# A four-layer gated transformer on one core: half of the expert gates spread by DMA instead of by TensorE

## What is computed

```python
x = x + tanh(g_xattn[L]) * attention_L(layernorm(x), ctx)
x = x + tanh(g_ffn[L])   * experts_L(layernorm(x))

# layer 0: 32 experts of width 64 (and 8 that do nothing), 6 of 40 per token
y = silu(x @ Wg.T) * (x @ Wu.T) @ Wd.T;        out += gate[e][:, None] * y
# layer 1: 16 experts of width 64, 2 per token, and a shared one of width 352
# layer 2: 31 experts of width 128, 3 per token, and a shared one of width 128
h = gelu(x @ W1 + B1);                         out += gate[e][:, None] * (h @ W2 + B2)
# layer 3: 8 experts of width 256 with relu, 2 per token
# layer 3's attention alone takes an integer mask over (query, key)
```

## Time and profile before

| | |
|---|---|
| runs shown, median (range) | 738.41 us (736.62 to 739.43) |
| the profiled execution: its own time | 738.34 us |
| its span | 736.5 us |
| PE busy | 652.4 us, 89% of the span |
| DVE busy | 531.7 us, 72% |
| ACT busy | 378.5 us, 51% |
| POOL busy | 270.8 us, 37% |
| DMA | 28.50 MB, mean 39 GB/s |
| spread matmuls, L675 | 150, first and last in the expert stages of layers 0 and 3 |

### The profile page before, as it was taken

The page is one execution under the profiler, slowest core; times in us unless marked ns, Lnnn a source line. Parts: engine busy times, 40 slices in busy tenths (PEclk is TensorE's granted clock), DMA queues, the critical chain, the costliest instruction groups (busy, mean ns, idle before and its releaser), DMA issues.

```text
span 736.5 us, 11957 instructions
## 1 busy us (share of the span) xinstructions
PE 652.4 (89%) x3653; PEld 457.8 (62%) x3653; DVE 531.7 (72%) x1298; ACT 378.5 (51%) x652; POOL 270.8 (37%) x463
## 2 busy tenths in 40 slices
PE   2787679998899988998999899999988899979997
PEld 2575547775676655675566546777766676645764
DVE  5482788887877537987864569888877988544886
ACT  1544254543467632553466337777744565622774
POOL 7723356663210003363111216666742000020673
PEclk9997689999999998999999999999999999998999
DMA  8211042110000010010000301111100010100111
GB/s 284 92 73 72 0 157 73 43 44 0 2 4 31 18 59 0 23 44 11 1 4 21 99 0 38 36 43 43 37 7 1 4 32 3 32 0 1 37 43 36
DMA packets 24087, 28.50 MB, mean 39 GB/s; under 512 B 4002, under 2 KB 19938, under 8 KB 24036
## 3 DMA queue, kind: packets, MB, share of 16 engines
q1 hardware_dynamic: 24036, 27.87, 12.2%
HBM read 22.22 MB, written 5.24 MB: 37 GB/s over the span
## 4 chain that ended last, share of the span: by engine, by line
PE 68%; DVE 20%; ACT 4%; issue 4%; POOL 2%; DMA 1%; DVEq 0%; SPq 0%; ACTq 0%; POOLq 0%
PE PS L653 10%; PE PS L654 10%; PE PS L655 10%; PE PS L675 4%; PE PS L879 4%; PE PS L516 4%; PE PS L788 3%; PE PS L862 3%; DVE consts L1503 2%; DVE negmax L1497 2%; DVE qst L1457 1%; PE PS L894 1%; DVE hid_lo L1412 1%; PE PS L859 1%; DVE xn L1224 1%
## 5 line engine op out<-in xcount | busy, mean ns | idle before, releaser
L414 POOL TENSOR_TENSOR wpair<-ring,ones_col 128x128 fp32r<-128x128 f32 (+1 forms) x150 | 78.7, 525 | 139.2 <-PE PS L655 98.7
L1406 DVE TENSOR_TENSOR pT<-pT,PS 128x512 f32<-128x512 f32 x150 | 102.5, 684 | 28.7 <-ACT pT L1050 22.8
L1149 ACT ACTIVATE pT<-PS 128x512 f32<-128x512 f32 x160 | 92.1, 592 | 49.2 <-PE PS L862 39.7
L1412 DVE TENSOR_TENSOR hid_lo<-pT,hid_hi 128x512 fp32r<-128x512 f32 x150 | 112.0, 746 | 2.3 <-ACT hid_hi L1057 1.4
L416 POOL TENSOR_TENSOR wpair<-ring,wpair 128x128 fp32r<-128x128 f32 (+1 forms) x150 | 103.5, 690 | 11.7
L1057 ACT ACTIVATE hid_hi<-pT 128x512 fp32r<-128x512 f32 x150 | 93.8, 625 | 12.4 <-DVE pT L1406 12.1
L653 PE MATMUL PS<-hid_hi,wpair 128*128 128x512 f32 x150 | 86.6, 577 | 5.8 <-DVE hid_lo L1412 5.8
L653 PE MATMUL PS<-xhi,wpair 128*128 128x512 f32 x204 | 85.3, 418 | 2.5 <-DVE pT L1406 1.9
L1050 ACT ACTIVATE pT<-PS,ring 128x512 f32<-128x512 f32 x96 | 65.9, 689 | 36.6 <-PE PS L655 36.6
L654 PE MATMUL PS<-xlo,wpair 128*128 128x512 f32 x204 | 82.5, 404 | 0.0
L655 PE MATMUL PS<-xhi,wpair 128*128 128x512 f32 x204 | 82.4, 404 | 0.0
(11 more groups left out here) (239 smaller groups left out, 1289.6 us busy)
## 6 DMA issues: line engine op xcount, KB each, us to landing
ring<-in_mlp SPq DMA_DIRECT2D x48, 128.5 KB, 2.1
ring<-in_glu SPq DMA_DIRECT2D x27, 192.0 KB, 2.4
keys<-qst SPq DMA_DIRECT2D x18, 256.0 KB, 2.0
kz<-keys SPq DMA_DIRECT2D x36, 128.0 KB, 3.1
qst<-kfull SPq DMA_DIRECT2D x96, 4.0 KB
...
```

The costliest lines, as they stand in the source:

```text
L1149: act.activation(pT[:, w % 8, :], PS[:, 2 + w % 2, :], ACT.Exp, scale=sc).then_inc(A["p"], 1)
L1406: dve.tensor_tensor(hid[:, hf, :], src[:, hf, :], PS[:, 6 + hf, :], ALU.mult).then_inc(M["hid"], 1)
L1412: dve.tensor_tensor(hid_lo[:, kept, :], hid[:, kept % 2, :], hid_hi[:, kept, :].bitcast(f32), ALU.subtract).then_inc(M["lo"], 1)
```

## The change

From entry 2 on in every layer, the gate of the second token half no longer comes through a spread matmul.

- PE transposes the second half's rows of `wtab` as f32 (4 transposes into bank 7, right after the old ones), ACT copies them out as `gate_rows` (32 rows of 512), between its copy of `wT` and its first activation.
- SP waits for `gate_rows`, writes them to DRAM, waits until that has landed, and then brings a row back onto 64 partitions with each DMA, two per entry: for entries 2 and 3 at once, and for entry e+4 right behind the ring load of that entry. These waits and DMAs stand ahead of `stack_keys` and of the mask loads on SP.
- DVE's multiplication of odd units from entry 2 on reads the gate from SBUF (`gate_slot`) and not from PSUM. Even units, and entries 0 and 1, stay as they were. That leaves out 14, 9, 30 and 14 spread matmuls in layers 0 to 3, 67 in all.
- `start_results` (the old L697 and L701) moves from ahead of the first spread to behind up(2) and spread(2). PE's second spread waits for `gate_rows`.
- The masks are prepared in six pieces, one behind each of units 24 to 29 of layer 0 (of 32), and no longer in layer 1's routing. `negk` moves into `ctx_tok`.
- The filler before `turn_weights` goes from 30 to 22 matmuls in layer 1, stays 30 in layer 2 and goes to 15 in layer 3.
- Some loads share a semaphore (`ld_gate` goes into `ld_bias`, `ld_out1` to `ld_out3` into `ld_out`, `kz_set` into `set_pool`); the loads stay as they were.

```diff
+        gate_rows = pT[0:EP, 7, :]
+        gate_own = sb("gate_own", [P, HALF])
+        gate_slot = [consts[:, C_DFT:C_DFT + HALF], consts[:, C_DFT + HALF:C_DFT + 2 * HALF], consts[:, C_BAND:C_BAND + HALF],
+                     gate_own[:, :]]
+        gd = [nc.dram_tensor(f"gates{L}", (EP, HALF), f32, kind="Internal").ap() for L in range(4)]
...
-        negk = sb("negk", [P, TB, S], bf16)
+        negk = ctx_tok[:, 6:8, :].rearrange("p a n -> p (a n)").bitcast(bf16).rearrange("p (k n) -> p k n", k=TB)
...
+        rows_out, rows_saved = sem("rows_out"), sem("rows_saved")
+        gate_in = [sem(f"gate_in{k}") for k in range(RING)]
+        by_pe = 2
+        gates_before = [[sum(len([e for e in range(by_pe, ROUTE[M]["ENT"]) if e % RING == k]) for M in range(L))
+                         for k in range(RING)] for L in range(4)]
...
+                def spread_gate(e, k):
+                    for side in range(2):
+                        row = gd[L][bass.ds(2 * e + side, 1), :] if glu else gd[L][bass.ds(e, 1), :]
+                        sp.dma_start(gate_slot[k][side * 64:side * 64 + 64, :],
+                                     row.broadcast_to([64, HALF])).then_inc(gate_in[k], 16)
+
                 if L == 0:
                     save_keys()
+                sp.wait_ge(rows_out, L + 1)
+                sp.dma_start(gd[L], gate_rows[:, :]).then_inc(rows_saved, 16)
+                sp.wait_ge(rows_saved, 16 * (L + 1))
+                for e in range(by_pe, RING):
+                    spread_gate(e, e)
...
                         sp.dma_start(ring[:, k, 0:cols], w[RING * i + RING + k, :, :]).then_inc(ring_in[k], 16)
+                        spread_gate(RING * i + RING + k, k)
                 for e in range(n - n % RING, n):
                     sp.wait_ge(M["y"], 2 * (e - RING) + 2 + UP_AHEAD)
                     sp.dma_start(ring[:, e % RING, 0:cols], w[e, :, :]).then_inc(ring_in[e % RING], 16)
+                    spread_gate(e, e % RING)
...
+                    pe.wait_ge(kv_out, len(chunks))
+                for i in range(4):
+                    mm = pe.transpose(PS[0:EP, 7, i * P:(i + 1) * P], wtab[:, 4 + i, :], ident)
+                mm.then_inc(rt["tr"], 1)
...
-                    keep_busy(7, 30)
+                    keep_busy(7, (0, 22, 30, 15)[L])
                 turn_weights(L)
-                for hf in range(NHALF):
-                    if glu:
-                        mm = pe.matmul(PS[:, hf, :], zerob[:, 0:P], zerob[:, :], start=True, stop=False,
-                                       skip_group_check=True)
-                    else:
-                        for j in range(PARTS):
-                            mm = pe.matmul(PS[:, hf, :], b2part[L][:, j, :], wT[:, hf * HALF:(hf + 1) * HALF],
-                                           start=(j == 0), stop=False, skip_group_check=True)
-                    mm.then_inc(M["y"], 1)
+                def start_results():
+                    for hf in range(NHALF):
+                        if glu:
+                            mm = pe.matmul(PS[:, hf, :], zerob[:, 0:P], zerob[:, :], start=True, stop=False,
+                                           skip_group_check=True)
+                        else:
+                            for j in range(PARTS):
+                                mm = pe.matmul(PS[:, hf, :], b2part[L][:, j, :], wT[:, hf * HALF:(hf + 1) * HALF],
+                                               start=(j == 0), stop=False, skip_group_check=True)
+                        mm.then_inc(M["y"], 1)
+
                 if glu:
                     pe.wait_ge(astep, (1, 4)[L])
                 if L == 0:
                     pe.wait_ge(kv_out, len(chunks))
-                for hf in range(NHALF):
-                    spread(hf, 0, hf)
+                spread(0, 0, 0)
+                pe.wait_ge(rows_out, L + 1)
+                spread(1, 0, 1)
                 for u in range(2 * RING):
                     up(u + 2, u // 2 + 1, (u // 2 + 1) % RING, u % 2)
-                    spread(u + 2, u // 2 + 1, u % 2)
+                    if u % 2 == 0 or u // 2 + 1 < by_pe:
+                        spread(u + 2, u // 2 + 1, u % 2)
+                    if u == 0:
+                        start_results()
...
                             up(u + 2, RING * i + k + 1, (k + 1) % RING, hf)
-                            spread(u + 2, RING * i + k + 1, hf)
+                            if hf == 0:
+                                spread(u + 2, RING * i + k + 1, hf)
...
-                act.wait_ge(rt["tr"], L + 1)
+                act.wait_ge(rt["tr"], 2 * L + 1)
                 act.activation(wT[:, 0:HALF], PS[0:PARTS * EP, 1, 0:S].bitcast(bf16), ACT.Copy).then_inc(rt["wT"], 1)
+                act.wait_ge(rt["tr"], 2 * L + 2)
+                if L > 0:
+                    act.wait_ge(rows_saved, 16 * L)
+                act.activation(gate_rows, PS[0:EP, 7, :], ACT.Copy).then_inc(rows_out, 1)
...
-                if L == 1:
-                    prepare_masks()
...
-                    dve.wait_ge(M["spread"], u + 1)
-                    dve.tensor_tensor(hid[:, hf, :], src[:, hf, :], PS[:, 6 + hf, :], ALU.mult).then_inc(M["hid"], 1)
+                    gate = PS[:, 6 + hf, :]
+                    if slot is None:
+                        dve.wait_ge(M["spread"], u + 1)
+                    elif hf == 0:
+                        dve.wait_ge(M["spread"], entry + by_pe + 1)
+                    else:
+                        gate = gate_slot[slot]
+                        dve.wait_ge(gate_in[slot], 32 * turn + 32 * (gates_before[L][slot] + (slot >= by_pe)))
+                    dve.tensor_tensor(hid[:, hf, :], src[:, hf, :], gate, ALU.mult).then_inc(M["hid"], 1)
...
+                    unit(u, u % KEPT, u // 2, u // 2 % RING, turn=u // 2 // RING)
+                    if L == 0 and u < 2 * RING * groups(n) + 6:
+                        prepare_masks(u - 2 * RING * groups(n))
...
+            def prepare_masks(step):
+
+                if step == 0:
+                    dve.wait_ge(ld_mask, 32)
+                    link(dve.tensor_scalar(negq[:, :, :], mask_i[:, 0, :, :], 0.0, NEG, ALU.is_equal, ALU.mult))
+                elif step == 1:
+                    link(dve.tensor_scalar(negk[:, :, :], mask_i[:, 1, :, :], 0.0, NEG, ALU.is_equal, ALU.mult))
+                elif step == 2:
+                    link(dve.tensor_scalar(maskedT[:, :, :], mask_i[:, 1, :, :], 0.0, None, ALU.is_equal))
+                elif step == 3:
+                    link(dve.tensor_scalar(maskq_f, mask_i[:, 0, :, :], 0.0, None, ALU.is_equal))
+                elif step == 4:
+                    link(dve.tensor_reduce(negfloor[:, :], maskq_f, AX.X, ALU.max))
+                else:
+                    link(dve.tensor_scalar(negfloor[:, :], negfloor[:, :], -3.0e37, 3.0e37, ALU.mult, ALU.add))
+                    dve.tensor_scalar(negfloor[:, :], negfloor[:, :], -MASKED / SCALE[3], None, ALU.max).then_inc(masks_ready, 1)
```

More of the change, by code:

```diff
@@ L448, in split_query_weights @@
             def split_query_weights(L):
-                pool.wait_ge(ld_out[L], 32 if L == 2 else 48)
+                pool.wait_ge(ld_out, 16 * 8)
                 if L > 1:
@@ L1390, in add_input, with unit @@
                                                       in1=x[:, i, :], op0=ALU.mult, op1=ALU.add))
-                def unit(u, kept, hf_first=False, first=False):
+                def unit(u, kept, entry, slot, turn=0, hf_first=False, first=False):
                     hf = kept % 2
@@ L1415, in experts @@
                 for u in range(2 * RING):
-                    unit(u, u % KEPT, hf_first=(u < 2), first=(u == 0))
+                    unit(u, u % KEPT, u // 2, None if u // 2 < by_pe else u // 2 % RING, hf_first=(u < 2), first=(u == 0))
                     add_input(u)
```

48 lines of the change are left out of this document (19 added, 29 removed).

## The result

The kernel before takes 738.11 us (median of 4 runs, 736.62 to 739.43), the changed one 751.81 us (4 runs, 749.59 to 753.90): a ratio of 1.0186, 95% interval 1.0145 to 1.0226. It is slower by 1.9%, where I had forecast 730 us and a range that ended at 738. The profiled execution took 749.59 us, its span is 747.5 us (before 736.5).

A forecast was written before the change was run, and what follows sets the result against it. PE was taken as the bound, busy without a gap in the expert stages. From the profiled 738.34 us, +2.3, -2.7, -2.4 and -5.7 us for layers 0 to 3 gave 729.8, stated as 730 us; range 724 to 738.

The forecast's parts named there:

- Both still fit: Expert stages: DVE's work per unit, 1.33 and 1.97 us, stays under PE's new steps of 1.495 and 2.185 us.
- part 1: Expert stages: 67 spreads of 0.23 us leave PE, saving 15.4 us if nothing else becomes the bound.
- +0.1 us for DVE: Odd units: where the SBUF multiplication meets POOL, DVE takes 0.1 us more and POOL 0.33 us; both hidden, no term.
- POOL locks DVE out: Rival, layers 0 and 1: odd multiplications wait for a whole POOL operation; 0.36 us per entry, +8.3 us, 738 us; chance 0.05.
- Part 4: SP's queue behind the wait for `gate_rows`: ring load late, PE begins entry 4 +3.1 us in layer 0, +4.8 in layer 2.
- The masks: +2.0 us: End of layer 0: mask pieces make DVE late by 2.9 + 0.7 - 8 x 0.2 = 2.0 us, bounds 0 and 4.
- Part 3: Filler and masks before the expert stages: layer 1 came out at -2.7 us and layer 3 at -5.7 us, spreads included.
- The filler term: Before layer 3's transposes: 15 fillers end with the routing at 672.4, where 30 ended at 675.5: -3.1 us.
- The weight loop becomes the bound: Rival, POOL's wait for ring loads in layers 2 and 3: +12.8 us, 742.6 us or more; chance 0.11.
- Filler and masks cost more: Rival: PE's clock falls to 1.2 GHz in layer 3 (3 us), or masks hold DVE longer (2 us): 735 us; chance 0.14.
- gates come late: Rival: DVE waits for gate DMAs, each asked for eight units ahead, so over 12 us late; chance under 1 in 50.
- my two signs of being wrong: PE waits for POOL at every second entry, or the stalls before entry 4 in layers 0 and 2 are absent.

The follow-up runs named there:

- experiment 2: Changed kernel with four slots for `hid`, so DVE waits for its subtraction of three units back: 741.65 us, ratio 1.0056 to the kernel before.
- 3: Kernel before the change with four slots for `hid`: 737.67 us, ratio 0.9990.
- experiment 1: Changed kernel with the odd gate multiplication reading PSUM (stale values), all DMAs kept: 744.38 us, ratio 1.0072 to the kernel before.
- experiment 10: Changed kernel with `kz` last, four `hid` slots and the odd multiplication reading PSUM: 725.12 us, ratio 0.9816 to the kernel before.
- 9: Changed kernel with `kz` behind the last ring load and four `hid` slots, masks still in layer 0: 732.77 us, ratio 0.9934 to the kernel before.
- 5: Changed kernel with `kz` and mask loads issued ahead of the wait for gate rows: 748.87 us, ratio 1.0171 to the kernel before.
- 6: Changed kernel with `kz` issued behind the last ring load of its layer: 746.15 us, ratio 1.0096 to the kernel before.
- experiment 4: Changed kernel with all gate DMAs and waits, but PE makes all spreads and DVE reads PSUM: 749.41 us, ratio 1.0142 to the kernel before.
- 7: Changed kernel with the masks back in layer 1's routing, not in layer 0: 755.26 us, ratio 1.0231 to the kernel before.
- 8: Changed kernel with `kz` and mask loads last, masks split over layers 1 and 2, two `hid` slots: 744.30 us, ratio 1.0082 to the kernel before.
- 11: Changed kernel with `kz` and mask loads last, masks split over layers 1 and 2, four `hid` slots: 729.77 us, ratio 0.9869 to the kernel before.
- 12: Kernel before the change with only the filler counts set to 22, 30 and 15: 734.13 us, ratio 0.9947.

## Why the prediction was wrong

By layer, the way to it included, I had forecast +2.3, -2.7, -2.4 and -5.7 us for layers 0 to 3; the profiled run has +7.8, -2.3, +7.2 and -1.8.

**"Both still fit" (part 1) is the step that failed.** I compared DVE's busy time per unit, 1.33 us, with PE's new step of 1.495 us. Busy time is not what a step of DVE takes: its instructions overlap by some 0.09 us, and the wait for its own last instruction adds 0.19 us that no busy share holds. The trace of before shows it: one gate multiplication starts 1.61 us after the last, and the idle time between had 0.04 to 0.13 us to spare, 0.10 in the mean. PE's step was to fall by 0.115 us. Experiments 2 and 3 show the cause: without the self-wait a unit falls from 1.693 to 1.514 us in the change, and by nothing in the kernel before. That holds for layers 2 and 3. In layer 0 four slots give 1.0 us or less; there the multiplication from SBUF is what didn't fit: from unit 10 to unit 24 a unit took 2.28 us in the change, 2.24 with four slots, and 2.18, PE's own step, with the operand in PSUM (1). In layer 1 both did fit: 2.18 us.

**The term "+0.1 us for DVE" in an odd unit was too small and in the wrong place.** The extra 0.155 us (0.721 to 0.876) lies on every subtraction, and 0.05 to 0.14 us more on each odd multiplication. By the medians the operand costs 7.4 us with the self-wait (experiment 1) and 7.7 us without it (10 against 9), by the stages alone 8.3 and 5.1. My rival "POOL locks DVE out" had a price of 8.3 us and a chance of 0.05. That the price comes so near is luck: its place was layers 0 and 1, and half of what was measured lies in layer 2. The rule of the Trainium skill ("SBUF — State Buffer", on the two separate sides) says that a DVE operation with two SBUF inputs and a GpSimd one that reads SBUF hold the shared port for a whole instruction. The trace agrees in kind: POOL's copy takes 0.392 us at its shortest in the change and 0.842 to 0.855 us in all 41 instances of experiment 2. I had read the 0.78 us of one subtraction as all that a meeting costs; it was one meeting in a stream where DVE had time left. That the subtraction stays at 0.817 us in experiment 1, with no more such operations than before, isn't the DMA traffic: experiment 10 has the same operations and DMAs, with four slots, and 0.707 us. The cause stays open; DVE no longer waits for PE in experiment 1, and may meet POOL at other moments.

**Together these are layer 2's steady state.** 1.693 us measured less the 1.495 of my sum, 0.198 us for the 56 units from entry 4 on, are 11.1 us, against 6.4 us of spreads: +4.7 us. The other 3.4 of its 8.1 us are the start, and experiments 5 and 6 gave 3.5 back.

**Part 4, the queue, was right in its mechanism.** Gates until 105.05 us (I said 105.0), ring load of entry 4 at 116.19 (114.0: the two mask loads took 2.3 us, not 1.2, and SP came 0.9 us after them), PE at 121.38 (121.1). That the last two agree is luck: the load was issued 2.2 us later than I said, and PE began 5.2 us behind it where I had kept the 7.2 of before; the load landed after 3.6 us, not 5.2. The stall of 3.64 us less the 0.52 of before is my +3.1. In layer 2 I said 4.8 us; 2.7 us were seen, 4.4 us where PE kept its pace (experiment 4), and 3.5 us came back when the queue was cleared (5, 6). Counted from the stage's first transpose, the ring load was issued after 13.9 us, as I had said, and PE began entry 4 after 17.6 us (13.4 before): +4.2. What I left out is the clock: behind the stall in layer 0 PE ran at 1.2 GHz, 6 matmuls fewer in 6 us, 1.4 us more.

**The masks: +2.0 us was somewhat too little, within its bounds of 0 and 4.** Their seven instructions took DVE 4.0 us in layer 0 (0.69, 0.68, 0.42, 0.62, 0.68, 0.42, 0.52 us) instead of the 2.7 us of layer 1. Without them layer 0 is 3.3 us (7), 4.6 (8) and, 11 against 9, 2.6 us shorter; in the stretch where they lie, from unit 23's subtraction to unit 31's, it is 2.7, 3.3 and 2.9 us. So of the 8 x 0.2 us of slack that I took off some 0.8 to 1.4 us were there; in experiment 4, where PE makes every spread, nearly all the 2.8 us that they took there were hidden. Layer 0 without queue and masks stands at 78.9 us (8); I had expected 2.3 below the kernel before. That is 0.9 below the 79.8 of before, but experiments 3 and 12, which change nothing there that counts, have 78.7 and 78.8 us: no gain is shown.

**Part 3: layer 1 was right** (-1.7 on the way and -0.6 in the stage, I said -2.7). **Layer 3 was not:** -1.8 us against -5.7. Its 14 spreads gave nothing, by part 1's step; with four slots the stage falls from 56.3 to 53.5 us. The filler term itself was right: from the first filler to the transposes PE took 4.2 us where it had taken 7.3, the 3.1 less that I had said. But the routing ahead of it ended 1.1 us later, so the way is 2.0 us shorter, and 3.7 in experiment 12. A stretch at 1.2 GHz lies ahead of these transposes in every profile, before too. With 15 fillers the way took 126.2 to 127.6 us in the three profiles where the stretch is short (4, 10, 12), and 128.0 to 128.4 us in the others, so I take that difference for the clock's and not for the change's.

**The rivals.** "The weight loop becomes the bound" was to end slower, at 742.6 us, and by another cause: in layer 2's steady part ring loads landed in 2.0 to 2.2 us, and experiment 4 with all the DMAs keeps the old pace. "Filler and masks cost more" held for the masks. That gates come late was never seen. Neither of my two signs of being wrong showed: PE waited for POOL at no second entry, and both stalls were there. No rival and no sign looked at DVE's step in layer 2; what did fail to appear were the steps of 1.61 and 1.38 us in turn.
